# A Mamba scan fed from six PSUM banks: transposes of u moved behind the additions, output projections moved four steps later, products taken two states at a time

## What is computed

```python
delta = softplus(einsum('blr,er->ble', dbc[..., :16], dtw) + dtb)
dA = exp(delta[..., None] * -exp(a_log))            # (B, L, 512 channels, 16 states)
mi = delta[..., None] * Bm[:, :, None, :] * xb[..., None]
# for each time step t:
v = 0.6 * v + mi_t
h = dA_t * h + v
y_t = einsum('ben,bn->be', h, C_t)
# afterwards
y = (ys + dp * xb) * silu(z)
out = einsum('ble,de->bld', y, ow)
```

## Time and profile before

| | us |
|---|---|
| median of 3 runs | 1562.31 |
| lowest, highest | 1557.7, 1563.35 |
| profiled execution, own time | 1557.23 |
| its span | 1555.7 |
| Mamba block in it, first to last scan | 76.59 to 975.66 |

### The profile page before, as it was taken

The page is one execution under the profiler, slowest core; times in us unless marked ns, Lnnn a source line. Parts: engine busy times, 40 slices in busy tenths (PEclk is TensorE's granted clock), DMA queues, the critical chain, the costliest instruction groups (busy, mean ns, idle before and its releaser), DMA issues.

```text
span 1555.7 us, 46788 instructions
## 1 busy us (share of the span) xinstructions
PE 1372.8 (88%) x20442; PEld 978.6 (63%) x20442; DVE 1065.9 (69%) x1347; ACT 905.5 (58%) x1365; POOL 920.7 (59%) x802
## 2 busy tenths in 40 slices
PE   4679799989899999999899888779989887999997
PEld 2357577767777767777677766434434344499986
DVE  4289798888799788788877887576666771422223
ACT  3758668757767757767766765126555565434440
POOL 1169878979979969969969986520303000035541
PEclk8799999999999999999999998979999999999999
DMA  4111221222222212221212344460514100612225
GB/s 133 50 47 66 84 82 58 85 83 85 84 84 84 84 57 84 84 84 57 110 57 80 128 135 125 79 139 1 93 30 87 22 1 23 257 48 68 69 65 179
DMA packets 41497, 127.26 MB, mean 82 GB/s; under 512 B 8784, under 2 KB 21584, under 8 KB 32848
## 3 DMA queue, kind: packets, MB, share of 16 engines
q1 hardware_dynamic: 34736, 108.27, 21.7%
q0 software_dynamic: 6048, 14.95, 3.7%
q10 hardware_dynamic: 512, 1.05, 0.4%
HBM read 97.90 MB, written 9.57 MB: 69 GB/s over the span
## 4 chain that ended last, share of the span: by engine, by line
PE 54%; DVE 14%; POOL 14%; issue 11%; ACT 5%; DMA 2%; DVEq 0%; SPq 0%; ACTq 0%; POOLq 0%
PE psum L631 8%; POOL hst L987 8%; PE psum L610 6%; DVE hst L783 5%; PE psum L1298 4%; PE psum L1710 4%; PE psum L1722 4%; PE psum L601 3%; PE psum L515 3%; POOL w_early L987 3%; PE psum L1280 2%; PE psum L1652 2%; PE psum L1264 2%; DMA overlay<-x_hat,origin 2%; DVE nmax L1419 2%
## 5 line engine op out<-in xcount | busy, mean ns | idle before, releaser
L987 POOL TENSOR_TENSOR hst<-hst,cb 128x512 f32<-128x512 f32 x399 | 515.9, 1316 | 121.6 <-DVE hst L783 106.8
L783 DVE TENSOR_TENSOR_SCAN hst<-dA,psum 128x512 f32<-128x512 f32 x399 | 467.2, 1205 | 134.4 <-PE psum L631 134.0
L610 PE MATMUL psum<-ident,hst 128*128 128x128 f32 x1596 | 234.3, 282 | 13.9 <-POOL hst L987 11.1
L610 PEld LDWEIGHTS psum<-ident,hst 128*128 128x128 f32 x1596 | 175.0, 142 | 63.7 <-issue 27.1
L923 ACT ACTIVATE dA<-delta,alog 128x512 f32<-128x512 f32 x256 | 176.9, 718 | 60.9 <-DVE hst L783 42.7
L923 ACT ACTIVATE dA<-xres,alog 128x512 f32<-128x512 f32 x256 | 176.2, 718 | 48.1 <-DVE hst L783 37.6
L1419 DVE TENSOR_REDUCE nmax<-psum 128x2 f32<-128x1024 f32 x128 | 154.6, 1220 | 58.7 <-PE psum L1264 58.4
L1348 ACT ACTIVATE pT<-psum 128x1024 f32<-128x1024 f32 x128 | 128.0, 1023 | 104.5 <-PE psum L1284 80.7
L631 PE MATMUL psum<-filt,c_early 64*64 64x86 f32 (+1 forms) x6144 | 148.6, 242 | 22.9 <-DVE hst L783 12.6
L631 PEld LDWEIGHTS psum<-filt,c_early 64*64 64x64 f32 x6144 | 126.9, 136 | 59.3 <-issue 43.6
L987 POOL TENSOR_TENSOR w_early<-w_early,cb 128x512 f32<-128x512 f32 x113 | 145.3, 1300 | 24.0 <-DVE w_early L783 23.7
(11 more groups left out here) (236 smaller groups left out, 2176.8 us busy)
## 6 DMA issues: line engine op xcount, KB each, us to landing
cb<-c_rows SPq DMA_DIRECT2D x64, 1024.0 KB, 4.8
qk_first<-w_early SPq DMA_DIRECT2D x64, 64.0 KB, 2.4
qk<-part SPq DMA_DIRECT2D x64, 64.0 KB, 2.6
w_up<-up_dram SPq DMA_DIRECT2D x8, 512.0 KB, 7.8
w_down<-down_dram SPq DMA_DIRECT2D x8, 512.0 KB, 13.0
w_up<-y_choice SPq DMA_DIRECT2D x8, 512.0 KB, 6.7
qk<-part POOLq DMA_DIRECT2D x48, 64.0 KB, 5.2
qk_first<-part SPq DMA_DIRECT2D x40, 64.0 KB, 2.4
```

Source lines behind the costliest of these rows:

```text
L610: m = pe.matmul(psum[:, Y0 + et % EP, t * P:(t + 1) * P], hst(i)[:, t * P:(t + 1) * P], ident[:], start=n == 0 and t == 0, stop=n == NSTAT ...
L783: dve.tensor_tensor_scan(hst(i), a, v, 0.0, ALU.mult, ALU.add).then_inc(scan_done, 1)
L987: pool.tensor_tensor(h, h, cb[:, q % 2, state_of(i)[1] % GN, :], ALU.mult).then_inc(g_done, 1)
```

## The change

- `u` is no longer in `TILED`: its 64 transposes come behind the addition of their own step instead of directly behind v.
- ScalarE copies the carries `mid`, `c`, `ch` at the even step at which TensorE makes them, one decay earlier in its program than before.
- The output projections `bo` move from steps 11, 13, 15, 16 to steps 15, 17, 18, 19 of the next period (those made in period 7 and behind it stay where they are).
- LAG is 8 instead of 7, so `hst` has ten tiles. The back end, which starts at LAG-2, and the middle shift by one step.
- GpSimd multiplies two tiles at once (128x1024) at even steps, after both scans.
- ScalarE writes its unused squares into `xs` instead of a tile of their own, with one more wait, for the transposes of `xs`.

```diff
-TILED = ("u", "mid", "c", "ch")
+TILED = ("mid", "c", "ch")
...
-            NDA, AHEAD, LAG, NRING, Y0 = 5, 4, 7, 6, 6
+            NDA, AHEAD, LAG, NRING, Y0 = 5, 4, 8, 6, 6
...
+            def hst_pair(i):
+                j = i % NH // 2 * 2
+                return hst_own[:, j:j + 2, :] if j < NH - 2 else spare[:, 0:2, :]
+
             def hst(i):
-                j = i % NH
-                return hst_own[:, j, :] if j < NH - 2 else spare[:, j - (NH - 2), :]
+                return hst_pair(i)[:, i % 2, :]
...
-                put(51, "act", "mid", 0)
+                put(50, "act", "mid", 0)
...
-                        put(53 + 2 * c, "act", part, c)
+                        put(52 + 2 * c, "act", part, c)
...
-                    s = s + 1 if at == "last" else ((17, 19, 21, 23) if at == NI - 1 else (11, 13, 15, 16))[t]
+                    s = s + 1 if at == "last" else ((17, 19, 21, 23) if at == NI - 1 else (15, 17, 18, 19))[t]
...
+                        act.wait_ge(bank_full, filled(k - 1, "xn", KD - 1))
...
-                    act.activation(square[:], xm[:, b * TB + j, :], ACT.Square, accum_out=stat[:, b * TB + j, 10:11]).then_inc(sq_done, 1)
+                    act.activation(xs[:, j, :], xm[:, b * TB + j, :], ACT.Square, accum_out=stat[:, b * TB + j, 10:11]).then_inc(sq_done, 1)
...
-                    h = hst(i)
-                    pool.wait_ge(scan_done, i + 1)
-                    pool.tensor_tensor(h, h, cb[:, q % 2, state_of(i)[1] % GN, :], ALU.mult).then_inc(g_done, 1)
+                    if i % 2 == 0:
+                        h, n = hst_pair(i), state_of(i)[1] % GN
+                        pool.wait_ge(scan_done, i + 2)
+                        pool.tensor_tensor(h, h, cb[:, q % 2, n:n + 2, :], ALU.mult).then_inc(g_done, 2)
```

More of the change, by code:

```diff
@@ L214, in build @@
             carry_id = sb(mc, "carry_id", [P, NSTATE])
-            square = sb(mc, "square", [P, D])
             xnT = lay(KD * S).rearrange("p (k s) -> p k s", k=KD)
```

## The result

Four runs of the changed kernel have a median of 1596.62 us (1592.98 to 1599.86), beside 1560.01 for the kernel before: ratio 1.0245, 95% interval 1.0221 to 1.0268. The profiled execution took 1593.99, 36.8 more than the 1557.23 of before. The forecast was 1582 with a range of 1567 to 1600.

What follows compares the result with a forecast made beforehand. TensorE's program, its work and its waits, was taken to set the pace. Terms 21 + 4 - 9 + 3 + 1 = +20 us, added to the median 1562.3, gave 1582; range 1567 to 1600.

Steps and rivals of the forecast that it cites:

- heels: TensorE's v waiting for its predecessor's scans to free a bank; such a step pair was said to take 3.73 us.
- Carries, +21: Scans 52 to 62: five v a period wait for their predecessor's scans, 111.9 us against 90.8, a loss of 21.
- u, +4: Transposes of u, scans 44 to 50: three v wait for predecessors' scans, a loss of 4 us, between 3 and 9.
- Output projections, -9: Scans 8 to 20: later projections lose the gate wait and half clock, a gain of 9 us, bounds -15.5 and -4.
- Scans 20 to 28, +3: v(26) waits for its predecessor's scans in five periods, partly filled by delta projections: a loss of 3 us.
- Two products at once, +1: GpSimd's paired products save it some 3 us a period without setting the pace; 1 us lost at the very end.
- Rival 1: GpSimd had held TensorE back and new waits for predecessors' scans cost nothing: 1538 us, chance 15%.
- Rival 2: Gain and loss cancel: carries +18, u +3, projections -15.5, scans 20 to 28 nothing; 1569 us or less, chance 15%.
- Rival 3: TensorE's clock falls in the carries, two half-clock stretches a period over six periods, +19: 1601 us, chance 13%.

Runs made afterwards that it cites:

- e2: The changed kernel with v alternating between banks 0-1 and 2-3 and side pieces in 4 and 5: 1571.55 us, ratio 1.0079.
- g3: The kernel before with only the output projections moved, to steps 15, 17, 18, 19: 1564.21 us, ratio 1.0022.
- e4: The changed kernel with the output projections of periods 1 to 6 back at steps 11, 13, 15, 16: 1615.23 us, ratio 1.0373.
- e1: The changed kernel with GpSimd's products taken one state at a time again: 1571.53 us, ratio 1.0092.
- f3: The changed kernel with old projection steps, u directly behind v and old carry copies, keeping LAG 8 and two-state products: 1612.19 us, ratio 1.0341.
- f5: The changed kernel with each state's GpSimd product cut into two of 128x256: 1605.79 us, ratio 1.0320.

## Why the prediction was right in sign and short in size

The heels are shown to be a cause (e2, g3, e4), and so is the hold (e1, f3). The 1596.62 lies within the range of 1567 to 1600, but above the 1574 to 1594 that the forecast itself had, and the sum reached the sign with one large cause missing. That it stayed within the range is partly luck: without that cause (e1, 1571.5) the kernel would have been 10 us faster than forecast.

- **Carries, +21:** 20.8 measured, at 3.71 to 3.72 a pair. Right. The cause is the later projections' effect on the banks, not anything done to the carries.
- **u, +4:** 2.8, at the lower bound of 3: the three pairs keep the pitch of 3.71 there too (66.79 in all). It is near what the stretch takes without heels (64.4 in e2, 71.1 in e4), so the heels at 46 to 50 cost little.
- **Output projections, -9:** 12.8 gained, within the bounds of -15.5 and -4. Scans 8 to 20 take 27.7 a period, to be set beside the forecast 28.3; the 27.6 was that less one `xd` of 0.65, which comes in from ahead of scan 8. That `xd` is missing there in turn: scans 0 to 8 are 4.1 shorter in all. There is no gate wait and no low clock. The mechanism was right and the gain 4 larger. What the later places are worth depends on the rest of the kernel: with LAG 8, whose gates come a step later, going back to the old ones costs 37.4 in scans 0 to 20 (e4).
- **Scans 20 to 28, +3:** 12.0. With single products (e1) it is 4.0, and v(26) waits 0.54 in five periods there, 2.7 in all, so the mechanism given for it was right and the rest is the hold, 8.0, of which some 2.4 is that even periods, where the clock falls behind scan 24, take 0.8 more than odd ones.
- **Two products at once, +1:** this is the step that failed. Its price on GpSimd was right (2.375 us, forecast 2.38; a period has 32 pairs, so the "26 us x 0.1" should read 32 x 0.1, 3.2), the additions wait for products about as long as before (11.6 us against 12.5), and yet it costs 25.1 us. I asked who waits for the product's end by a semaphore and not what else runs while it lasts. The sum thus put VectorE's lengthening at nothing. The trace of before held the evidence: a 128x192 product on VectorE of 1251 ns beside taps of 128x510 at 749, and in period 0 an operation of 128x8 that took 3.50 us and ended at 174.67, with the third GpSimd instruction in a row:

```profile
169.91 2.49 POOL L987 TENSOR_TENSOR hst<-hst,cb 128x512 f32<-128x512 f32 x2
171.17 3.50 DVE L756 TENSOR_SCALAR stat<-stat 128x8 f32<-128x8 f32 x1
172.36 1.05 POOL L959 TENSOR_TENSOR filt<-toep,bcol 128x516 f32<-128x516 f32 x1
173.38 1.25 POOL L987 TENSOR_TENSOR hst<-hst,cb 128x512 f32<-128x512 f32 x1
```

- **Scans 28 to 44, not in the sum:** +9.9, and with single products -6.4. The table has v(40) on the heels in every period before and in none after; TensorE stood 0.33 to 0.41 ahead of v(40) and 0.66 ahead of v(42), whose bank an `xd` had yet to read, in each period before, 6.2 us in six, and stands for neither in e1. Part of this gain only moved across step 44: over scans 28 to 50 e1 is 1.5 below before.
- **The sum without the hold:** e1 was 9.4 us longer over periods 1 to 6 than before (684.3 - 674.9), where the terms summed to 19; the projections and scans 28 to 44 are the difference. The term left out added 22.5 there.
- **Rival 1** (heels covered) is refuted: in the carries each costs its 3.72 pitch. **Rival 2** (they cancel) is what g3 shows for the projections by themselves, -12.7 and +16.1; for the whole change it fell. **Rival 3** (the clock) is refuted: the carries run at a granted 1.00, and the low stretches are three in periods 1 to 6, as before; they moved from the gate to scan 24 or so of the even periods, behind a v that had waited 1.41. In periods 3 and 5 the same v waits 1.41 too and no low stretch follows. Here are the carries of period 1 and the low stretch of period 2:

```profile
302.54:321.11 18.57, 12.85 (x322) 9.96 (x315) 11.66 (x11) 14.40 (x31) 16.27 (x10) 1.00 0.27 101
...
373.41:376.82 3.41, 3.41 (x56) 2.89 (x51) 2.44 (x3) 2.37 (x5) 1.78 (x1) 0.50 0.27 108
```

On the profiled execution's 36.8: periods 1 to 6 make 31.9, period 0 3.8, period 7 -1.0; the block began 2.5 later, which no part of the change explains (its start lies between 76.4 and 82.5 in the kernels here). Together they are 37.2.

## What to carry to other kernels

Ask of an instruction that gets longer not only who waits for its end, but what else runs on the neighbouring engine while it lasts: two short GpSimd products instead of one long one were worth 1.6% here (and halving them once more cost 2.2%). When pieces are moved in a program whose buffers go round by age, write the table of who gets whose buffer before and after; it foretold 20.8 us to within one, and where the sum didn't follow it (v(40)), 6 us went unforeseen. And a wait (the gate) can grow when a slowness elsewhere is mended, so try both together: bank rule 1572, later projections 1564, both 1547.

## What the runs showed of the hardware

Some VectorE operations whose tensors are all in SBUF are held while a GpSimd product runs. Those that start at least 0.08 us before the product's end get done a fixed time after it, somewhat less than what they take alone (changed kernel, e1 and f5; the three long holds of f5 are counted from the last instruction that held them):

| VectorE operation | alone, us | ends after the product's end by |
|---|---|---|
| 128x192 product, two SBUF tensors | 0.36 | 0.21 to 0.23 |
| 128x512 clip, one SBUF tensor | 0.39 to 0.43 | 0.28 to 0.32 |
| 128x512 maximum, two SBUF tensors | 0.66 to 0.69 | 0.55 to 0.60 |

So what a hold costs is what is left of the product when the operation starts. Longer products can leave more, but how much they do depends on where in them the operations fall. Median and longest duration in ns beside products of 128x256, 128x512 and 128x1024 (f5, e1, changed kernel; for the taps and the scan, the mean):

| VectorE operation | 128x256 | 128x512 | 128x1024 |
|---|---|---|---|
| 128x192 product | 358, 3366 | 1442, 1449 | 2478, 2483 |
| maximum (xres) | 769, 4759 | 680, 1504 | 828, 2732 |
| maximum (delta) | 772, 4745 | 819, 1290 | 1113, 2736 |
| clip (xres) | 506, 818 | 404, 677 | 414, 1472 |
| clip (delta) | 516, 815 | 402, 674 | 400, 1470 |
| 128x510 taps, with one tensor in PSUM | 749 | 749 | 749 |
| 128x512 scan, with one tensor in PSUM | 1204 | 1205 | 1203 |

The Trainium skill, SBUF — State Buffer, section "Who interferes with whom", states this: a VectorE instruction with two SBUF inputs contends with a GpSimd instruction that reads SBUF, one in a 2-port mode with GpSimd too, and whichever comes first has the shared ports for its whole instruction while the other waits. By that rule the bend product should get its turn when the GpSimd product ends and the taps should not notice; the trace agrees on both, with 0.22 us between the two ends at 488.53. By the rule taken alone VectorE's turn would come at the end of the first product; in the three long holds of f5, and in the 3.50 us of the kernel before, VectorE got it only after two to five more GpSimd instructions that followed each other without a gap, and no run here shows why.

It goes the other way too. In f5 a 128x256 product that starts during one of these operations, behind the product that held it, ends 0.59 us after the operation, where alone it takes 0.72. One that starts 0.34 before a clip ends took 0.92:

```profile
489.26 0.81 DVE L699 TENSOR_SCALAR xraw<-xres 128x512 f32<-128x512 f32 x1
...
489.73 0.92 POOL L991 TENSOR_TENSOR hst<-hst,cb 128x256 f32<-128x256 f32 x1
```
